# Softmax attention of a two-layer macaron kernel: bf16 thirds on the whole array exchanged for float32r halves on two row tiles

## What is computed

```python
B, S, D, H = (2, 256, 128, 16)                  # HD = D // H = 8; the input x is (1, 2048, 128)
qkv = jnp.einsum('bsd,ed->bse', x, qkv_w) + qkv_b
scores = jnp.einsum('bhqe,bhke->bhqk', q, k) * scale      # 16 heads, 2048 queries, 2048 keys
attn = jax.nn.softmax(scores, axis=-1)
out = jnp.einsum('bhqk,bhke->bhqe', attn, v)
```

## Time and profile before

| what | us |
| --- | --- |
| executions shown, median | 1883.17 |
| span of the profiled execution, its own time | 1880.9 |
| PE busy in the span | 1635.9 |
| DVE busy | 1354.7 |
| ACT busy | 836.9 |
| first unit's first pass, alone (218.3 to 264.2) | 45.90 |
| second passes of the 16 units, with the other first passes (264.2 to 1037.5) | 773.30 |

### The profile page before, as it was taken

How to read it: one execution, slowest core, us unless ns; L and a number is a source line. 1 busy time by engine, 2 the same in 40 slices (tenths; PEclk the granted TensorE clock), 3 DMA queues, 4 the chain that set the end, 5 groups by cost and what they waited for, 6 DMA issues and landing times. The chain is left out here.

```text
span 1880.9 us, 23731 instructions
## 1 busy us (share of the span) xinstructions
PE 1635.9 (87%) x7285; PEld 683.8 (36%) x7285; DVE 1354.7 (72%) x1951; ACT 836.9 (44%) x1493; POOL 222.4 (12%) x145
## 2 busy tenths in 40 slices
PE   6987589999999999999998798899994356589999
PEld 3433112222222222222221443366661122256665
DVE  5776788888888778888880577666656999745654
ACT  2433427777676666667778253322223000042222
POOL 2222300000000000000000022211101324301110
PEclk8998659999999999999999899899996777799999
DMA  6000400011001100111000000000000000000000
GB/s 168 2 0 1 135 16 8 14 27 40 9 14 28 30 12 7 27 30 24 2 2 2 1 1 0 1 1 0 0 1 0 0 0 1 0 1 6 6 5 7
DMA packets 32021, 29.49 MB, mean 16 GB/s; under 512 B 7788, under 2 KB 27032, under 8 KB 31928
## 3 DMA queue, kind: packets, MB, share of 16 engines
q1 hardware_dynamic: 31928, 28.31, 5.9%
HBM read 22.13 MB, written 4.19 MB: 14 GB/s over the span
## 5 line engine op out<-in xcount | busy, mean ns | idle before, releaser
L1382 DVE TENSOR_REDUCE mx<-ps 128x1 f32<-128x1024 f32 x512 | 605.2, 1220 | 147.5 <-PE ps L1269 143.2
L1269 PE MATMUL ps<-k,q 72*128 72x512 bf16 x1024 | 403.0, 408 | 11.4 <-DVE mx L1382 9.3
L1304 PE MATMUL ps<-q,k 84*128 84x512 bf16 x1024 | 346.8, 384 | 20.7 <-ACT xn L1359 14.5
L1359 ACT ACTIVATE xT<-ps 128x512 f32<-128x512 f32 x512 | 265.1, 603 | 156.7 <-PE ps L1304 156.6
L1359 ACT ACTIVATE xn<-ps 128x512 f32<-128x512 f32 x512 | 266.2, 603 | 107.4 <-PE ps L1304 107.4
L1269 PEld LDWEIGHTS ps<-k,q 72*128 72x128 bf16 x1024 | 110.1, 115 | 331.4 <-DVE mx L1382 185.4
L854 ACT ACTIVATE silu<-ps 128x512 f32<-128x512 f32 x144 | 85.3, 596 | 265.3 <-PE ps L827 261.9
L1304 PEld LDWEIGHTS ps<-q,k 84*128 84x128 bf16 x1024 | 102.3, 102 | 185.6 <-ACT xn L1359 69.6
L889 DVE TENSOR_TENSOR hid<-ps,silu 128x512 f32<-128x512 f32 x144 | 97.8, 690 | 91.2 <-PE ps L831 89.6
L827 PE MATMUL ps<-xT,ew 128*128 (+1 forms) x288 | 151.0, 606 | 6.5 <-PEq L1750 4.8
L817 PEld LDWEIGHTS ps<-ew,hid 128*128 128x128 f32 x1152 | 138.7, 192 | 30.6 <-issue 29.9
(11 more groups left out here) (239 smaller groups left out, 1688.9 us busy)
## 6 DMA issues: line engine op xcount, KB each, us to landing
k<-k_parts SPq DMA_DIRECT2D x90, 64.0 KB
q<-q_parts SPq DMA_DIRECT2D x144, 32.0 KB
k<-k_parts SPq DMA_DIRECT2D x108, 32.0 KB
ew<-in_L_ffn_w_dram SPq DMA_DIRECT2D x2, 1024.0 KB
wraw<-in_L_ffn_w_dram SPq DMA_DIRECT2D x3, 512.0 KB, 6.7
q_parts<-part SPq DMA_DIRECT2D x4, 384.0 KB, 5.3
k_parts<-part SPq DMA_DIRECT2D x4, 384.0 KB, 2.6
v<-values SPq DMA_DIRECT2D x8, 144.0 KB, 4.2
```

The source lines that it names most:

```text
L1269: mm = nc.tensor.matmul(m.ps[:, S1B[i % 4], :], queries, k1[:, h, kc * CHUNK:(kc + 1) * CHUNK], start=True, stop=True)
L1304: nc.tensor.matmul(m.ps[:, S2_BANK[s], :], k2[:, h, kt * P:(kt + 1) * P], q[:, qc, h, :], start=True, stop=True).then_inc(s2_ready, 1)
L1359: nc.scalar.activation(ex[kt % P_RING][:, h, :], m.ps[:, S2_BANK[s], :], ACT.Exp).then_inc(exped, 1)
L1382: nc.vector.reduce_max(mx[:, h, qt, kc:kc + 1], m.ps[:, 2 * (i % 2):2 * (i % 2) + 2, :], AX.XY)\
```

## The change

- **Type and tiles.** q and k are kept as two float32r halves (the first rounded by ACT, the second the difference, by DVE) and no longer as three bf16 parts. Their four products take 32 contraction rows. Two heads lie side by side on the partitions, at 0 and at 64; row 32 is a row of zeros in q, and the halves of the negated maxima take 8 rows behind it. A matmul has 33 rows in the first pass and 41 in the second, and the two matmuls of a pair stand in row tiles 0 and 64 (64x128 tiles) of the array. The number of matmuls and their columns stay.
- **k1 and k2 become one `k`**, with two buffers, one group ahead; the values are read where they lie; there is no hardware loop.
- **Order.** A step has both second-pass pairs one behind the other, then a first-pass pair, the weighing, and a first-pass pair. Each pair has one wait and one count. `LEAD` is 6 of 32 places, `HOLE` 1.
- **DVE.** A reduction takes the same two banks (1024 elements a partition) and gives two maxima, not one. At the unit's end 4 instructions stand for 7.
- **SP.** The maxima go in 8 transfers of 8 rows and not in 4 of 12.
- **Start.** DVE clears row 32 of q for both tiles and `neg_part` ahead of the normalisation. ACT fills the rows behind row 32 of both k buffers, 4 instructions of 9 rows by 4096; PE's first pass waits for the first two.

```diff
-LEAD = 12
-HOLE = 3
+LEAD = 6
+HOLE = 1
...
-    q = m.sb("q", [ROWS_M, CHUNKS, GH, CHUNK], BF16, stack=kv_stack)
-    k1 = m.sb("k1", [ROWS, GH, T], BF16, stack=kv_stack)
+    q = m.sb("q", [P, CHUNKS, 2, CHUNK], F32R, stack=kv_stack)
+    k = [m.sb(f"k{i}", [P, 2, T], F32R, stack=kv_stack) for i in range(2)]
...
+            for b in range(2):
+                low = 64 * b + ROWS
+                nc.vector.memset(q_f[low:low + 1, :, :, :], 0.0).then_inc(zero_row, 1)
+            nc.vector.memset(neg_part_f, 0.0).then_inc(zero_row, 1)
             norm.all_chunks(step)
...
-                step(nc.vector.tensor_tensor(rest[:, :], full[:, n % 2, :], part[:, n % PART_RING, 0, :], ALU.subtract))
-                step(nc.vector.tensor_copy(part[:, n % PART_RING, 1, :], rest[:, :]))
-                nc.vector.tensor_tensor(part[:, n % PART_RING, 2, :], rest[:, :], part[:, n % PART_RING, 1, :], ALU.subtract)\
-                    .then_inc(parts_ready, 1)
-                dve.wait_ge(parts_ready, n + 1)
+                nc.vector.tensor_tensor(part[:, n % PART_RING, 1, :], full[:, n % 2, :], part_f[:, n % PART_RING, 0, :],
+                                        ALU.subtract).then_inc(parts_ready, 1)
...
+            def first_pass(u, i):
...
+                if u * SLOTS + i >= 2:
+                    pe.wait_ge(s1_used, u * SLOTS + i - 1)
+                for b in range(2):
+                    rows = slice(64 * b, 64 * b + OFF)
+                    queries = q[rows, qc, p, :].rearrange("r (p t) -> r t p", t=TPC)[:, qt, :]
+                    last = nc.tensor.matmul(m.ps[:, S1B[i % 2] + b, :], queries, k[g % 2][rows, p, kc * CHUNK:(kc + 1) * CHUNK],
+                                            start=True, stop=True)
+                last.then_inc(s1_ready, 1)
...
+            def scores(u, n):
...
+                for b in range(2):
+                    s = 2 * n + b
+                    if u * STEPS + s >= len(S2B):
+                        pe.wait_ge(exped, u * STEPS + (s - S2_SINCE[s] + 1))
+                for b in range(2):
+                    rows = slice(64 * b, 64 * b + ROWS_M)
+                    last = nc.tensor.matmul(m.ps[:, S2_BANK[2 * n + b], :], k[u // CHUNKS % 2][rows, p, kt * P:(kt + 1) * P],
+                                            q[rows, u % CHUNKS, p, :], start=True, stop=True)
+                last.then_inc(s2_ready, 1)
...
+            nc.tensor.matmul(m.ps[:, AVB, :], zeros[:, 0:P], zeros[:, :], start=True, stop=True)
+            pe.wait_ge(ones_stored, 2)
...
+            for u in range(UNITS):
                 for kt in range(TILES):
+                    scores(u, 2 * kt)
+                    scores(u, 2 * kt + 1)
+                    ahead(u, 2 * kt)
                     if kt >= 1:
+                        weigh(u, kt - 1)
+                    elif u >= 1:
+                        weigh(u - 1, TILES - 1)
+                    ahead(u, 2 * kt + 1)
...
+                    nc.vector.reduce_max(mx[:, 2 * p:2 * p + 2, qt, kc], m.ps[:, S1B[i % 2]:S1B[i % 2] + 2, :], AX.X)\
                         .then_inc(s1_used, 1)
```

More of the change, by code:

```diff
@@ L6 @@
 BF16 = mybir.dt.bfloat16
+F32R = mybir.dt.float32r
 ALU = mybir.AluOpType
@@ L1070, in _ @@
             written(0)
[L1071 to L1074 removed]
+            sp.wait_ge(zero_row, 3)
+            load_q(sp, 0, preloaded)
             write(2)
@@ L1200, in load_next_q @@
-            def load_next_q(g, qc, last):
-                if last and qc >= 1:
-                    return
-                u = g * CHUNKS + qc
-                if qc == 0:
-                    if not isinstance(g, int) or g > 0:
-                        sp.wait_ge(s2_ready, u * STEPS)
-                    load_q(sp, g, 3)
-                else:
-                    sp.wait_ge(s2_ready, u * STEPS)
-                    load_q(sp, g + 1, qc - 1)
-            load_maxima(0, 0)
-            for qc in range(CHUNKS):
-                unit(0, qc, False)
@@ L1216, in _ @@
-            with sp.Fori(1, GROUPS - 1) as g:
-                for qc in range(CHUNKS):
-                    unit(g, qc, False)
-            for qc in range(CHUNKS):
-                unit(GROUPS - 1, qc, True)
+                    rows = neg_turned_f[b * 32:b * 32 + HALVES * GH, :, :].rearrange("r j t -> r (j t)").unsqueeze(1)\
+                        .to_broadcast([HALVES * GH, 2, P])
+                    for half in range(2):
+                        sp.dma_start(q_f[64 * half + OFF:64 * half + ROWS_M, u % CHUNKS, :, b * P:(b + 1) * P], rows)\
+                            .then_inc(max_loaded, 16)
@@ L1280, in weigh @@
+            def weigh(u, kt):
+                if kt == 0 and u >= 1:
                     pe.wait_ge(out_stored, u)
@@ L1328, in _ @@
-            nc.tensor.matmul(m.ps[:, AVB, :], zeros[:, 0:P], zeros[:, :], start=True, stop=True)
-            for i in range(STEPS):
-                first_pass(0, 0, i)
-            for i in range(S1_IN[LEAD].start):
-                first_pass(0, 1, i)
-            unit(0, 0, False, True)
-            for qc in range(1, CHUNKS):
-                unit(0, qc, False)
-            with pe.Fori(1, GROUPS - 1) as g:
-                for qc in range(CHUNKS):
-                    unit(g, qc, False)
-            for qc in range(CHUNKS):
-                unit(GROUPS - 1, qc, True)
@@ L1341, in _, with ahead @@
-            weigh(GROUPS - 1, CHUNKS - 1, TILES - 1)
+            def ahead(u, n):
+                at = u + 1 + (n + LEAD) // SLOTS
+                if at < UNITS:
+                    for i in S1_IN[(n + LEAD) % SLOTS]:
+                        first_pass(at, i)
+            nc.tensor.matmul(m.ps[:, AVB, :], zeros[:, 0:P], zeros[:, :], start=True, stop=True)
+            pe.wait_ge(ones_stored, 2)
+            for i in range(SLOTS):
+                first_pass(0, i)
+            for i in range(S1_IN[LEAD].start):
+                first_pass(1, i)
@@ L1347, in store_out @@
                 act.wait_ge(av_done, (u + 1) * TILES)
-                nc.scalar.activation(outs[:, bass.ts(u, 1), :].rearrange("p u t -> p (u t)"), m.ps[:, AVB, :],
-                                     ACT.Copy).then_inc(out_stored, 1)
-            def unit(g, qc, last, first=False):
-                u = g * CHUNKS + qc
+                nc.scalar.activation(outs[:, u, :], m.ps[:, AVB, :], ACT.Copy).then_inc(out_stored, 1)
+            for i in range(2):
+                for b in range(2):
+                    low = 64 * b + ROWS
+                    nc.scalar.activation(k[i][low:64 * b + ROWS_M, :, :],
+                                         own_row[low:64 * b + ROWS_M, :].unsqueeze(2).to_broadcast([ROWS_M - ROWS, 2, T]),
+                                         ACT.Copy).then_inc(ones_stored, 1)
+            for u in range(UNITS):
                 for kt in range(TILES):
@@ L1404, in maxima @@
                 dve.wait_ge(max_turned, u + 1)
-            maxima(0, True)
-            with dve.Fori(1, UNITS) as u:
-                maxima(u)
+    kv_stack.close()
     m.stage()
```

310 lines of the change are left out of this document (113 added, 197 removed).

## The result

| | before | after |
|---|---|---|
| time, median of 4 runs (lowest to highest), us | 1884.33 (1879.5 to 1886.85) | 2399.81 (2396.06 to 2402.16) |
| ratio, 95% interval | | 1.2739 (1.2715 to 1.2762) |
| span of the profiled execution, us | 1880.9 | 2394.3 |
| mean granted clock of PE | 0.927 | 0.677 |

The changed kernel is 27% slower. The prediction, 1905 us with a range of 1845 to 1990, was wrong. The time is that of rival 4, the clock at half, which had 7%.

The account below looks back on a forecast made before the run. The prediction took the bound to change from the loop of PE and DVE to one of PE and ACT. Second passes +8, start +12 and clock +5 on a span of 1880.9 gave 1906, adjusted to 1905 us; range 1845 to 1990.

Parts of the forecast that it names:

- rival 4: Attention stage: the clock stays at half, all streams double, step near 4.9 us, result near 2370; 7%.
- The failed step: Clock at the start of the second passes: it rises as before, only later because of the gaps; 5 us.
- The step at full clock: Second-pass step, now a loop of PE and ACT: 3.03 us against 3.04 before.
- rival 3: Pairs do not run together, or float32r streams at half rate: step 3.79 us, result about 2095; 8%.
- rival 1: Short weight loads and no lag within a pair: step 2.79 to 2.87 us, result 1847 to 1867; 24%.
- the forecast's own case: The main forecast over the ends of weight load and pair lag: 1867 to 1949 us; 49%.
- the 8 in the sum: Second passes as a whole: 781 us against 773.3, so +8 us.
- The start: DVE's clearings 8.5 us, jobs giving back 3.5, ACT's uncovered fillings 7.0: +12 us, between +4 and +17.
- Rival 2: Transfers of the maxima at 0.78 us an issue: every unit starts 2.9 us late, result 1948; 12%.
- DVE idle for PE in each step: Sign in the changed profile: DVE idle, waiting for PE, for about 0.6 us of each step.
- PE's idle time before the second second-pass pair: Sign for the predicted wait between second-pass pairs: about 0.65 us idle in every step, released by ACT.
- PE waiting for the maxima in the first unit only: Sign at unit starts: with issues near 0.3 us, PE waits for the maxima only in the first unit.

Follow-up runs that it names:

- e12: e9 with the added products of zeros 33 rows high in place of 128; 2398.57 us.
- e7: The changed kernel with every pair of both passes issued twice into the same banks; 2786.39 us.
- e13: e10 with `LEAD = 9` in place of 6; 1974.27 us.
- e8: The changed kernel with 24 bf16 matmuls of zeros ahead of the second pass and 12 in its first step, in place of the missing weighing; 2383.52 us.
- e9: The changed kernel with two 128-row bf16 products of zeros between each step's second-pass pairs, except step 1 of a unit; 1978.74, 2011.81, 2101.67 and 2102.7 us.
- e11: e10 in the split order, with one product of zeros behind the first-pass pair; 2047 to 2154 us in four runs.
- e5: The changed kernel, float32r kept, with each pair matmul over 97 or 105 rows on the whole array, one after the other; 2207.33 us.
- e14: e9 with 9 output columns in place of 128 in the added 128-row products; 1983.99, 1986.72, 1986.87, 2058.49 and 2076.05 us.
- e10: e9 plus the 36 products of zeros of e8; three runs of 1988 to 1990 us and three of 2100 to 2106.
- e4: The kernel before, in bf16 at full height, with its scores of a step in the changed kernel's order and its wait for ACT; 2040.57 us.
- split order: The changed kernel with a first-pass pair between the two second-pass pairs of a step; with this edit alone 2305.57 us.

## Why the prediction was wrong

**The failed step is the clock.** The prediction says: "the clock rises at 273 after 8 us without a gap. The new steps have a gap of about 1 us each, so I count 5 us for a later rise." It took the rise as given and priced a delay. What those 8 us before had was not only no gap but products of 72 and 84 rows besides the weighing. The change replaced these by products of 33 and 41 rows. In the changed kernel the clock did not rise once in the 1270 us of second passes. Nor did it with a nearly unbroken stream (e12, 98% busy), and twice the pairs (e7) raised it for 3.4 us at a time. The term was about 499 - 66 = 433 us in place of 5, an estimate, with 66 what the second passes take more than before in e13 at full clock.

**Rival 4 had the right size and the wrong reason.** Its step of 4.9 is 5.00, its 2370 is 2400. But it argued from the busy share, "some 70%, that of the first unit's first pass". The rows that it names show another count: the first pass has PE busy for 2.61 of 3 us, 87%, and for 38.29 of 45.90, 83%, at 0.50. The changed step has 84% by the same count, no more than a stretch that stood at 0.50, so by the argument of the share itself this rival deserved more than 7%. And the runs show that the share alone doesn't decide (e12 at 98% and 0.50). Against it the prediction held that its unbroken stretches are longer; they are, and it didn't matter. The diff itself showed the rows go from 72 and 84 to 33 and 41, and no row of the trace had a stage built on such products at either clock. A property that the trace doesn't show was not bounded from both sides, as the load had been; bounding it so would have put more than 7% on this rival too. The Trainium skill, "TensorE: Matmul & The Clock Gate", Part 1 on the clock gate, says that "the default state is throttled, and activity releases the throttle". The trace agrees that the stage begins throttled (0.50 in its first pass, before and after the change). That activity of PE is enough to release it this case doesn't bear out: in e12 PE is busy for 1250 of 1270 us at 0.50.

**The step at full clock: right in form, 0.25 short in size.** Predicted and measured (e8's rows): first-pass pair with its load open 0.43 and 0.46; first second-pass pair to ACT 0.33 and 0.45; exponential and back to PE 0.64 and 0.71; second second-pass pair and first-pass pair to the weighing 0.64 and 0.69; weighing 0.97 and 0.97. The sum is 3.03 with rounding, measured 3.28. The load of float32r was nearly right (0.17 taken, 183 ns at the median in e9's rows); half of the miss is the way to ACT, read from bf16 products that each have a count of their own. Whether the type or the single count of a pair adds these 0.12 us, no run tells. The pair runs together, so rival 3 is out, and rival 1 (2.79 to 2.87) too.

**The sum, had the clock held.** e13's span is 90.9 us above that of before: 62 are the steps, seen in the stores 52.1 us apart in place of 47.9, 15 times; 24.5 lie ahead of the second passes, of which 7.3 are products of zeros; some 3 more are products of zeros in the first step. The other 1 or 2 lie at the last unit. Without the 36 products it would be some 1964 us: within the stated range, but above the 1949 at which the forecast's own case ended. So the likeliest sign, slower, would have been right, and the reason, a step bound by PE's wait for ACT, too; but the second passes would have cost some 63 us more in place of the 8 in the sum, so even then the size would have been right only with the help of the wide range.

**The start.** Predicted +12 less 1.5, measured +14.7. The clearings are 3.47 us each and not 4.3, but with the gaps at them little is won, and the 3.5 us that the jobs were to give back did not come: the attention stage begins at 226.06 in place of 218.33, +7.7. The fillings hold PE until 233.36, the predicted 7 us, of which the first pass makes good a part: from the stage's begin to DVE's last maximum it is 44.5 us in place of 39.3, +5.2. From there to PE's first score it is 8.4 in place of 6.6, +1.8: the transfers of the maxima take 2.5 more, DVE 0.7 less.

**Rival 2, the maxima.** Its price was nearly right: an issue is 0.69 us at the median (0.78 assumed), in place of q's 0.3, though it carries 16 rows where q's has 32.

```profile
L1145 SPq DMA_DIRECT2D q<-neg_turned x128: 685/686/1736, 271.7 to 1477.8; - x128
```

I had taken 0.33, since fewer rows should not cost more. In time it hurt far less than its 43 us: in e9 PE waits 4.7 us for maxima in all, 2.9 of them in the first unit and 1.8 before the last. The step is longer than assumed, which gives 0.7 us more room in three steps; the rest of the difference wasn't followed up. What it cost besides is the clock, which fell behind such waits in e11 and which no row of before could show.

**The other signs.** DVE idle for PE in each step: right. PE's idle time before the second second-pass pair, about 0.65: 0.79, with ACT to end it, so the central step of the argument held. PE waiting for the maxima in the first unit only: right at half speed, wrong at full. Stores near 49 us apart: 79.2, and by the prediction's own test, "wrong if the stores lie 46 or 60 us apart", it fell.

## What to carry to other kernels

Packing two small products side by side on TensorE saves stream time (0.9 us of a 4.2-us step here, e5 against e8), but count what it does to the height: here a stage with matmuls of 33 and 41 rows ran at half clock, even with PE busy for 98% of the time (e12). Before such a change, look in the trace for a stretch that is made of products of the new height and read its granted clock; where there is none, the clock is an unknown with both its levels in the range, and the double of PE's time is one end. If the clock is lost, products of zeros over all 128 rows in gaps that are there anyway can bring it back; in the gap they cost nothing here (3.27 us a step with them, 3.28 without), and together with a push at the start and a longer lead they gave back 425 of the 515 us. They don't do it reliably by themselves (1979 to 2103 us in e9).

## What the runs showed that I had not expected

- The width of the added products made no difference and their rows did: with 128 rows by 9 columns the clock rose in all five runs, with 33 rows by 128 in none of four (e14, e12).
- Yet 128-row products in every gap but one a unit stood at half for 218 and 335 us with PE busy for 99% and 96% (e14, e10).
- The changed step holds a raised clock for a whole unit (52 us, e8) and didn't raise it in 1194 us. The same instructions ran at 3.28 or 5.00 us a step, by what had run before them.
- bf16 in half-height tiles alternates between the levels where float32r stays down (clock 0.58 to 0.80 in windows of 100 us, against 0.50). Why the type matters stays open, as does what exactly tips a clock that is up.
- At full height float32r costs 4.18 us a step against 3.63 for bf16 with 72 and 84 rows in nearly the same order (e5, e4); tiles bring float32r to 3.28. The order costs 0.23 of that (3.28 against 3.05 in the split order).
- A DMA issue of the maxima on SP costs nearly the same for 16 rows of 128 elements as for 48: 0.69 us and 0.78.
